# First group's maxima in the projection, output sums on ScalarE and GpSimd, and a new cyclic order

## The reference, cut to what matters

```python
q = (x @ q_w + q_b).reshape(Bx, Tx, NH, HD).transpose(0, 2, 1, 3)
att = jnp.einsum('bhqd,bhkd->bhqk', q, k) * (1.0 / np.sqrt(HD))
att = att + build_alibi_bias(NH, Tx)[None]
att = jnp.where(causal[None, None], att, -jnp.inf)
att = jax.nn.softmax(att, axis=-1)
y = jnp.einsum('bhqk,bhkd->bhqd', att, v)
return y.transpose(0, 2, 1, 3).reshape(Bx, Tx, Cx) @ o_w + o_b
```

## Time and profile before

| what | value |
|---|---|
| median of 3 runs | 2517.78 us (2517.63 to 2517.99) |
| the profiled execution | 2520.94 us, span of its instructions 2519.2 us |
| granted PE clock over the span | 0.978 |
| PE, VectorE, ScalarE, POOL busy | 96%, 90%, 73%, 44% |
| first instruction of the attention stage | 859 us |

### The profile page before, as it was taken

The page is one execution under the profiler, slowest core; times in us unless marked ns, Lnnn a source line. Parts: engine busy times, 40 slices in busy tenths (PEclk is TensorE's granted clock), DMA queues, the critical chain, the costliest instruction groups (busy, mean ns, idle before and its releaser), DMA issues.

```text
span 2519.2 us, 64138 instructions
## 1 busy us (share of the span) xinstructions
PE 2419.7 (96%) x24840; PEld 1524.6 (61%) x24840; DVE 2254.9 (90%) x4278; ACT 1846.3 (73%) x3503; POOL 1104.6 (44%) x1432
## 2 busy tenths in 40 slices
PE   6779989999999799999999999999999999999998
PEld 4569989999999544545545455545454555454543
DVE  4568878888888699999999999999999999999992
ACT  2348868778777348787777787877877778778776
POOL 1145545555555214343453443544434535444344
PEclk9989999999999779999999999999999999999999
DMA  2015555555554533334244343342442443434422
GB/s 79 1 47 170 178 184 178 172 173 176 178 175 164 157 88 103 103 102 139 69 136 117 88 122 111 96 132 75 130 125 80 128 122 87 122 85 120 133 59 68
DMA packets 330088, 300.61 MB, mean 119 GB/s; under 512 B 111864, under 2 KB 280206, under 8 KB 329784
## 3 DMA queue, kind: packets, MB, share of 16 engines
q1 hardware_dynamic: 321704, 294.58, 38.7%
q10 hardware_dynamic: 8080, 1.94, 0.4%
HBM read 175.09 MB, written 118.49 MB: 117 GB/s over the span
## 4 chain that ended last, share of the span: by engine, by line
PE 52%; DVE 10%; issue 1%; ACT 1%; SPq 1%; DMA 0%; POOL 0%; POOLq 0%; ACTq 0%
PE t_y L1754 19%; PE t_a L1670 11%; PE t_r L1710 9%; PE t_r L1722 9%; DVE t_mxc L1843 8%; PE t_a L1697 4%; ACT t_prob L1782 1%; DVE t_ysw L1856 1%; DVE t_yT L1867 1%; SPq L117 0%; DVE t_rec L1860 0%; DMA t_km<-scr_k 0%; DVE t_mx L1850 0%; POOL t_res L1915 0%; SPq L104 0%
## 5 line engine op out<-in xcount | busy, mean ns | idle before, releaser
L1782 ACT ACTIVATE t_prob<-t_r 128x512 f32<-128x512 f32 (+2 forms) x2560 | 1220.7, 560 | 310.9 <-PE t_r L1722 271.3
L1843 DVE TENSOR_REDUCE t_mxc<-t_a 128x1 f32<-128x512 f32 (+3 forms) x2432 | 1430.5, 649 | 19.1 <-PE t_a L1670 15.1
L1670 PE MATMUL t_a<-t_km,t_qm 63*128 63x128 bf16 (+4 forms) x4608 | 683.9, 277 | 19.7 <-PEq L770 8.9
L1710 PE MATMUL t_r<-t_qm,t_km 51*128 51x512 bf16 (+3 forms) x3072 | 628.0, 326 | 4.2 <-ACT t_prob L1782 0.7
L1754 PE MATMUL t_y<-t_prob,t_v 128*32 128x512 f32 (+3 forms) x6144 | 627.9, 496 | 0.9 <-POOL t_prob L1920 0.9
L1722 PE MATMUL t_r<-t_q,t_k 58*128 58x128 bf16 (+4 forms) x4608 | 614.2, 270 | 0.0
L1670 PEld LDWEIGHTS t_a<-t_km,t_qm 51*128 51x128 bf16 (+1 forms) x4608 | 273.9, 94 | 536.3 <-DVE t_mxc L1843 426.8
L1920 POOL TENSOR_SCALAR_AFFINE_SELECT t_prob<-t_prob 128x512 f32<-128x512 f32 x512 | 323.9, 634 | 610.5 <-ACT t_prob L1782 608.9
L1722 PEld LDWEIGHTS t_r<-t_q,t_k 51*128 51x128 bf16 (+1 forms) x4608 | 323.0, 94 | 41.2 <-issue 0.3
L1710 PEld LDWEIGHTS t_r<-t_qm,t_km 51*128 51x128 bf16 x3072 | 234.7, 94 | 89.0 <-ACT t_prob L1782 60.3
L1754 PEld LDWEIGHTS t_y<-t_prob,t_v 128*32 128x32 f32 x6144 | 134.3, 108 | 165.9 <-issue 95.1
(11 more groups left out here) (209 smaller groups left out, 3788.5 us busy)
## 6 DMA issues: line engine op xcount, KB each, us to landing
scr_q<-j_part SPq DMA_DIRECT2D x96, 256.0 KB, 3.4
scr_k<-j_part SPq DMA_DIRECT2D x96, 256.0 KB, 2.6
t_qm<-scr_q SPq DMA_DIRECT2D x384, 64.0 KB
t_km<-scr_k SPq DMA_DIRECT2D x384, 64.0 KB
t_q<-scr_q SPq DMA_DIRECT2D x384, 64.0 KB
t_k<-scr_k SPq DMA_DIRECT2D x384, 64.0 KB
scr_v<-j_v SPq DMA_DIRECT2D x32, 544.0 KB, 5.0
t_v<-scr_v SPq DMA_DIRECT2D x64, 272.0 KB
```

What stands on the lines that cost most here:

```text
L1670: mm = pe.matmul(abank[n % A_SLOTS][:, at + lo:at + hi], q_main[z][part, h, i * P:(i + 1) * P], k_main[z][part, h, k0 + lo:k0 + hi], start ...
L1710: pe.matmul(ring[n % RING_BANKS][:, at * w:(at + 1) * w], k_main[z][part, heads[at], j * P:(j + 1) * P], q_main[z][part, heads[at], q0:q0 ...
L1782: nc.scalar.activation(prob[:, q % SLOTS, h0:h0 + m, 0:w], ring[n % RING_BANKS][:, 0:m * w].rearrange("p (h n) -> p h n", h=m), ACT.Exp).t ...
L1843: V.tensor_reduce(out, data, AX.X, ALU.max, negate=True).then_inc(s_au, 1)
```

## The change

The maxima of group 0 are computed in the projection, in steps 12 to 30, one entry of `MAX_UNITS` a step: PE computes it in both halves into the two banks that `turn0` uses, ahead of `q`, and VectorE reduces both banks in one instruction, between `x1` and `mix0`. For that the first group's loads come after step 3 instead of 6, and the keys of group 1 are loaded there too, so that the attention's own list of first loads starts with group 1's operands. POOL sets the maxima's tile instead of VectorE. In the attention, an output product is copied out of its slot by ScalarE, and POOL adds the residual to the copy; VectorE's addition is gone. Stores and residual loads wait for POOL's addition. The planner knows of both, and `CYCLE` is another order of the same 75 entries with other lags. In the old one the output products have the lags 6, 4, 6 and 5 (numbers 2, 0, 3 and 1), in the new one 4, 5, 6 and 5 (0, 1, 3 and 2).

```diff
@@ prepare: tiles and semaphores that live from the projection into the attention
+        keep(early, "t_qm1", [P, GH // 2, T], BF16)
+        keep(early, "t_km1", [P, GH // 2, T], BF16)
+        keep(early, "t_mxc", [P, 2, GH, 2 * QT])
...
-        for name in ("t_s_qkv0", "t_s_qk0"):
+        for name in ("t_s_qkv0", "t_s_qk0", "t_s_qk1", "t_s_first"):
@@ project: SP
                 load_marks(sp, a, scr, qm0, km0, s_qk0)
+                load_marks(sp, a, scr, qm1, km1, s_qk1)
                 load_constants(sp, a, scr, q0, k0, s_qkv0)
...
                 for e in range(2):
                     load_maxima(sp, a, scr, qm0, km0, 0, s_qk0, e)
+                for e in range(2):
+                    load_maxima(sp, a, scr, qm1, km1, 1, s_qk1, e)
...
-                    if m == 6:
+                    if m == 3:
                         first_group()
@@ project: TensorE
+            def first_maxima(u):
+
+                pieces, two = MAX_UNITS[u]
+                if u == 0:
+                    pe.wait_ge(s_qk0, 16 * (MARKS + MAX_LOADS))
+                at = 0
+                for h in two:
+                    for i, k0, w, near in pieces:
+                        far = w - P if near else w
+                        for depth, lo, hi in ((NMAIN, 0, far), (NMAX, far, w)):
+                            if lo < hi:
+                                for e in range(2):
+                                    part = slice(HALF * e, HALF * e + depth)
+                                    mm = pe.matmul(b_turn0[:, 512 * e + at + lo:512 * e + at + hi],
+                                                   qm0[part, h, i * P:(i + 1) * P], km0[part, h, k0 + lo:k0 + hi],
+                                                   start=True, stop=True)
+                        at += w
+                mm.then_inc(s_first_pe, 1)
...
-            for what, m in cycle([("turn1", 0), ("kv", -1), ("f0", 1), ("q", 0), ("k", 0), ("kk", 0), ("v", 0),
+            for what, m in cycle([("turn1", 0), ("kv", -1), ("f0", 1), ("max", 0), ("q", 0), ("k", 0), ("kk", 0), ("v", 0),
                                   ("turn0", 2), ("r", 0)]):
...
+                    if m - 2 >= FIRST_AT:
+                        pe.wait_ge(s_first, min(m - 2 - FIRST_AT + 1, len(MAX_UNITS)))
...
+                elif what == "max":
+                    if 0 <= m - FIRST_AT < len(MAX_UNITS):
+                        first_maxima(m - FIRST_AT)
@@ project: VectorE, one reduce over both banks for each unit
+                dve.wait_ge(s_first_pe, u + 1)
...
+                V.tensor_reduce(out, data, AX.X, ALU.max, negate=True).then_inc(s_first, 1)
...
             for what, m in cycle([("stats0", 0), ("xT_low", -1), ("x1_low", -2), ("ffn", -3), ("mix1", -2), ("x1", -1),
-                                  ("mix0", -2), ("mix_low1", -2), ("rest_q", -2), ("stats1", -1), ("mix_low0", -2),
+                                  ("max", -2), ("mix0", -2), ("mix_low1", -2), ("rest_q", -2), ("stats1", -1), ("mix_low0", -2),
                                   ("rest_k", -2), ("vbias", -2), ("ksq_low", -2)]):
@@ project: GpSimd
+            pool.memset(mxc[:, :, :, :], 3.0e38).then_inc(s_set, 1)
@@ the order and the planner
+FIRST_AT = 12
 CYCLE = (
-    ("max", 6, 2), ("max", 17, 1), ("pair", 17, 4), ("pair", 18, 4), ("max", 34, 2), ("max", 33, 2),
-    ("weigh", 8, 4), ("max", 13, 1), ("max", 22, 2), ("pair", 19, 4), ("max", 10, 2), ("pair", 0, 3),
-    ("max", 21, 2), ("pair", 1, 3), ("max", 2, 2), ("weigh", 9, 4), ("max", 9, 2), ("max", 14, 2),
...
+    ("max", 17, 2), ("pair", 17, 4), ("pair", 18, 4), ("max", 0, 1), ("max", 21, 1), ("weigh", 8, 4),
+    ("max", 8, 2), ("pair", 19, 4), ("max", 25, 2), ("max", 16, 1), ("pair", 0, 3), ("max", 15, 2),
+    ("pair", 1, 3), ("max", 12, 1), ("weigh", 9, 4), ("max", 19, 2), ("pair", 2, 3), ("max", 2, 2),
+    ("max", 7, 2), ("pair", 3, 3), ("weigh", 10, 4), ("weigh", 11, 4), ("max", 14, 2), ("max", 35, 2),
+    ("pair", 4, 3), ("out", 0, 4), ("out", 1, 5), ("out", 3, 6), ("pair", 5, 3), ("max", 22, 2),
+    ("max", 1, 2), ("pair", 6, 3), ("max", 18, 1), ("weigh", 0, 3), ("max", 37, 1), ("pair", 7, 3),
+    ("max", 24, 1), ("max", 5, 1), ("pair", 8, 3), ("max", 10, 1), ("weigh", 1, 3), ("max", 13, 0),
+    ("pair", 9, 3), ("max", 20, 1), ("max", 33, 1), ("pair", 10, 3), ("max", 36, 0), ("weigh", 2, 3),
+    ("rows", 0, 2), ("weigh", 3, 3), ("max", 23, 1), ("pair", 11, 3), ("pair", 12, 3), ("max", 28, 1),
+    ("max", 29, 0), ("weigh", 4, 3), ("out", 2, 5), ("max", 3, 0), ("max", 4, 0), ("weigh", 5, 3),
+    ("max", 11, 0), ("pair", 13, 3), ("max", 32, 1), ("max", 27, 1), ("pair", 14, 3), ("max", 30, 1),
+    ("weigh", 6, 3), ("max", 9, 1), ("pair", 15, 3), ("max", 34, 1), ("max", 31, 1), ("pair", 16, 3),
+    ("max", 26, 1), ("weigh", 7, 3), ("max", 6, 1),
 )
...
+    pl.done.update({("max", 0, u): 0.0 for u in range(NU)})
...
+    maxima_in(0)
     for rank, kind, t, x in cyclic():
+        if kind == "max" and t == 0:
+            continue
...
-            pl.give("DVE", end + 165, rank, ("sum", t, x), 616,
-                    last if all(("sum", t, n) in slot_freed for n in range(OUTS)) else None, "slot")
+            def summed(end, t=t, x=x, last=last):
+                pl.give("POOL", end, NG * t + 4.5, ("add", t, x), 1300,
+                        lambda end: last(end) if all(("add", t, n) in pl.done for n in range(OUTS)) else None)
+
+            pl.give("ACT", end + 165, rank, ("sum", t, x), 520, summed)
@@ attend: SP
-            first_keys(1)
             first_load(1)
             first_keys(2)
             first_keys(3)
...
-                    sp.wait_ge(s_au, used[last_out(t)])
+                    sp.wait_ge(s_add, max(added[t, n] for n in range(OUTS)))
                     sp.dma_start(outd[t], o[:, :, :]).then_inc(s_out, 16)
@@ attend: TensorE, the wait for a slot
+                elif before[0] == "out":
+                    pe.wait_ge(s_al, act_used["sum", before[1], before[2]])
@@ attend: ScalarE
+            def summed(b, x):
+                act.wait_ge(s_a, slot["out", b, x] + 1)
+                act.wait_ge(s_shift, shifts[b, 2 * x + 1])
+                nc.scalar.copy(o[:, 2 * x:2 * x + 2, :].rearrange("p t n -> p (t n)"),
+                               abank[slot["out", b, x] % A_SLOTS][:, 0:512]).then_inc(s_al, 1)
@@ attend: VectorE
+                if t == 0:
+                    dve.wait_ge(s_first, len(MAX_UNITS))
+                else:
+                    dve.wait_ge(s_au, used[last_max(t)])
...
-            def summed(b, x, n):
-                dve.wait_ge(s_a, n + 1)
-                dve.wait_ge(s_shift, shifts[b, 2 * x + 1])
-                V.tensor_tensor(o[:, 2 * x:2 * x + 2, :].rearrange("p t n -> p (t n)"), abank[n % A_SLOTS][:, 0:512],
-                                res[:, 2 * x:2 * x + 2, :].rearrange("p t n -> p (t n)"), ALU.add).then_inc(s_au, 1)
-
-            V.memset(mxc[:, :, :, :], 3.0e38)
@@ attend: GpSimd
+            def add(b, x):
+                pool.wait_ge(s_al, act_used["sum", b, x])
+                mine = o[:, 2 * x:2 * x + 2, :]
+                pool.tensor_tensor(mine, mine, res[:, 2 * x:2 * x + 2, :], ALU.add).then_inc(s_add, 1)

```

More of the change, by code:

```diff
@@ L1555, in attend @@
         slot = {e: n for n, e in enumerate(in_slot)}
-        first_max = [min(slot["max", t, u] for u in range(NU)) for t in range(GROUPS)]
-        used = [sum(e[0] != "rows" for e in in_slot[:n + 1]) for n in range(len(in_slot))]
+        first_max = [None] + [min(slot["max", t, u] for u in range(NU)) for t in range(1, GROUPS)]
+        used = [sum(e[0] == "max" for e in in_slot[:n + 1]) for n in range(len(in_slot))]
+        act_used = {e: n + 1 for n, e in enumerate(e for e in ORDER["ACT"] if e[0] in ("lift", "sum"))}
+        added = {(t, x): n + 1 for n, (t, x) in enumerate(e[1:] for e in ORDER["POOL"] if e[0] == "add")}
         in_ring = [e for e in ORDER["PE"] if e[0] == "pair"]
@@ L1633, in _ @@
                     if t > 0:
-                        sp.wait_ge(s_au, used[last_out(t - 1)])
+                        sp.wait_ge(s_add, max(added[t - 1, n] for n in range(OUTS)))
                         sp.wait_ge(s_out, 16 * t)
@@ L1814, in _ @@
                     spread(t)
+                elif what == "sum":
+                    summed(t, x)
                 elif what == "yhigh":
@@ L1846, in join @@
                 z = t % 2
-                dve.wait_ge(s_au, used[last_max(t)])
+                if t == 0:
+                    dve.wait_ge(s_first, len(MAX_UNITS))
+                else:
+                    dve.wait_ge(s_au, used[last_max(t)])
                 if t > 1:
@@ L1896, in _ @@
                                         ALU.subtract).then_inc(s_ow, 1)
-                elif what == "sum":
-                    summed(t, x, slot["out", t, x])
         @block.gpsimd
@@ L1962, in _ @@
                     shift(t, x)
+                elif what == "add":
+                    add(t, x)
 def kernel(**inputs):
```

50 lines of the change are left out of this document (31 added, 19 removed).

## The result

The changed kernel takes 2540.70 us (median of four runs, 2538.72 to 2540.93), beside 2517.86 us for the one before (four runs, 2517.63 to 2517.99): a ratio of 1.0087, 95% interval 1.0075 to 1.0098. It is slower by 22.8 us. The forecast was 2505.6 us, in a range from 2487 to 2523, with a chance of 0.15 for slower. The prediction was wrong in sign and its range missed. The profiled execution has a span of 2538.7 us where that of before has 2519.2, so 19.5 us have to be found in the trace.

A forecast was written before the change was run, and what follows sets the result against it. VectorE was taken to bound the attention stage, with PE 3 us behind and full in the projection. Terms +7.5 +10.6 -12.5 -19 +1.2 = -12.2 us against the median 2517.78 gave 2505.6 us, range 2487 to 2523.

The forecast's parts named there:

- Part 1: First group's maxima in the projection: 19 units +7.5 us, the reduce hidden on VectorE, SP's longer block +10.6 us.
- Part 2: Start of the attention: first exponent at 896.3 instead of 908.83 us, -12.5 us, with group 2's keys late.
- Part 3: Output products' additions taken off VectorE: attention period 98.9 instead of 100.1 us, -19 us, and +1.2 us at the end.
- It is one short operation a group: Joining of the maxima on VectorE, 0.61 us once beside busy POOL: blocking by GpSimd was given no cost.
- So VectorE bounds the stage now, PE stands 3 us behind it: Attention stage, old order: period 100.14 us, VectorE needs 99.2, PE an estimated 96.2, 1 us lost between them.
- a stack of 98.3: Least attention period in us, new order, taking the slower of PE and VectorE in each group; 0.6 of loss added.
- PE's stack of 96.8 us: Estimate of PE's work in one attention period, new order, packed half by half from durations between starts.
- The end (+1.2 us): After the last output product, a copy and a POOL addition (1.9 us) replace one addition of 0.69 us.
- Rival (c): PE sets the attention period, above 100.0 us, and the projection's costs decide: 2525 or 2530 us; chance 10%.
- rival (b): The attention period hardly moves, 99.5 to 100.0 us: 2515 to 2523 us; chance 19%.
- (a): VectorE alone bounds the attention: period 97.3 to 98.0 us, -43 to -33, 2482 to 2492 us; chance 16%.
- (d): VectorE's reduce isn't hidden in the projection: +23 us, 2529 us; chance 5%.

The follow-up runs named there:

- the mended kernel: The changed kernel with the one-input joining, SP's load block cut into eight pieces and group 2's keys issued ahead of group 1's operands: 2495.42 us, ratio 0.9903.

## Why the prediction was wrong

**Part 1 held.** The units cost 7.8 us (7.5 said), the reduce nothing, and SP's block 9.4 more (10.6 said). The new issues took 10.4 us of queue time, nearly as said; the block grew by 9.1 only, since the first group's own operand loads at its end were issued in 6.1 us instead of 7.4. The mechanism was right down to the engine that stands.

**Part 2 held.** -12.9 us (-12.5 said), with a gap of 13.92 us on VectorE ("some 14"), behind the late keys; group 2's keys issued first made it 4.44 us, as that reading says.

**Part 3 failed, in two steps.** Forecast was a period of 98.9; it is 101.30. From the first exponent to the end the forecast had -19 +1.2 us and the trace has +17.8, 35.6 us apart. The first step below accounts for 19.9 of these (what the joining with one input took away) and leaves the other 15.7 to the second.

The first failing step is the sentence "It is one short operation a group". It is one short operation, but it isn't short when it meets GpSimd: it lasts until GpSimd's instruction has ended, up to 1.15 us instead of 0.18. The prediction had the one instance of before (0.61 us at 2466.82) in hand and asked neither how long it could get nor whether the change moves GpSimd's work onto it. GpSimd's instruction at that place is a masking, and the joining ended 0.04 us after it:

```profile
2466.74 0.64 POOL L1920 TENSOR_SCALAR_AFFINE_SELECT t_prob<-t_prob 128x512 f32<-128x512 f32 x1
```

The bound from rows stood there: the longest two-input instruction of GpSimd beside it is 1.27 us, four joinings a period, up to 4.4 us a period. What ran was 1.80 us a period on VectorE, 1.34 of it in the period and 19.9 us in the whole. That is a rival with a place, a price and a sign, and it was missing from the list. The Trainium skill ("SBUF — State Buffer", Who interferes with whom) says that a VectorE instruction with two SBUF inputs is blocked while a GpSimd instruction reads SBUF; the trace of after agrees 29 times, and in the mended kernel 29 joinings with one input begin inside the same subtraction and take 0.20 to 0.21 us. One joining doesn't fit: in the kernel before, at 965.67 us, it began 0.03 us after the subtraction had and took 0.17 us. The prediction weighed that rule by the count of instructions instead of by how long one can wait.

The second is "So VectorE bounds the stage now, PE stands 3 us behind it". The loss "between them" was set at 0.6 us over a stack of 98.3; with the joining mended the loss over that stack is 1.65 us (99.95). The chain of waits of before had shown whose stage it is: over 1200 to 1600 us 82% of it is PE. VectorE's 0.9 us of idle time in a period says that it is nearly full, not that its work sets the pace. Taking 3.8 us a period from PE shortened the period by 2.11 us; taking 2.45 from VectorE, in the old order, lengthened it by 0.5, and with an order fitted to it shortened it by 0.3. PE's stack of 96.8 us did not bear "3 us behind". Whether the stack itself is short or the loss between two uneven engines is larger than the 0.6 us allowed isn't settled: an output product alone takes PE 1.62 us where 1.52 was said, and the passes and the changes of layout were not measured one by one. The end (+1.2 us) can't be told apart in a stage total of 1608.7 us.

The Trainium skill ("Perfetto Trace Analysis", Identifying the Most-Contended Engine) asks for the share of the peak rate and the busy share of weight loads. The first is not worked out here; by the second, 197 of 400 us in the mended kernel, TensorE would be at half its limit. But PE holds 76% of the chain there, and the run with fewer matmuls shows that this is real. Here the measurement decides against reading the weight loads alone, as the prediction had it; it only drew too little from that.

Rival (c), PE sets the period and the projection's costs decide, gave 2525 to 2530 us. The time came out above it, and by another way. What it had right is that PE's side takes back what the additions gave. With the joining out of the way the kernel came to rival (b)'s numbers (2515 to 2523 us at a period of 99.5 to 100.0), at their upper edge: 2523.15 us at 99.96. The rest up to 2540.7 us is the joining. Rivals (a) and (d) are out: the period is far from 97.3, and the reduce is hidden.

Three things stay open. Why the old order with the copies and additions moved idles 3.49 us a period, more than the 0.90 plus the 2.45 taken off, is not explained. Nor is why moving three output products by three entries costs 2 us a period. In both, ScalarE's exponents hold 2.5% of the chain from 1200 to 1600 us, where the kernel beside each has 1.0% and 1.5%; that fits copies standing ahead of exponents on ScalarE, but no run tests it alone. And the block's cutting was tested together with the load order; the two are told apart by their marks in one run (the longest step, the first exponent), not by two runs.

## What to carry to other kernels

Before moving elementwise work to GpSimd, list VectorE's instructions with two SBUF inputs, however short, and price each at the length of the longest GpSimd instruction that may run beside it, a masking as well as an addition. A reduce over pairs of one tile does the same work with one input and was immune here. When two engines are both nearly full, take the one that holds the chain of waits over several periods for the likely bound, and test it by removing work from that one alone. A long block of issues on a shared queue costs whatever waits behind the store at its end: here the step that held it was 18.1 us longer for nothing but its being in one piece.

## What was not expected of the hardware

A VectorE minimum over 32 columns (0.18 us alone) that starts while GpSimd's subtraction of 1.27 us runs ends 0.04 to 0.05 us after that one, 29 times of 29 in the changed kernel. The same values reduced through one input of 64 columns take 0.20 to 0.22 us, in the middle of GpSimd's instruction or alone. Neither the busy share nor an idle time gives this away: a stretched instruction counts as busy, with 0.0 idle before it. In these views only the mean duration of its group (601 ns beside 179) does.
